# An attention and FP4 feed-forward block on one core: softmax row sums written to PSUM, the bias of q added in its copy, one copy moved from VectorE to ScalarE, and three PSUM banks in place of four

## What is computed

```python
mod = (silu(c) @ wmod).reshape(32, 6, 1, 128)            # sa, ca, ga, sb, cb, gb
h = layernorm(x) * (1 + ca) + sa
q, k, v = ((h @ W + b).reshape(b, 16, 8, 256) for each)
attn = softmax(einsum('bhdt,bhds->bhts', k, v) * temperature)
x = x + ga * einsum('bhdt,bhts->bhds', q, attn).reshape(b, 256, 128)
h = layernorm(x) * (1 + cb) + sb
# fp4_linear: both operands are rounded to FP4 in blocks of 16
hid = silu(fp4_linear(h, w_gate)) * fp4_linear(h, w_up)
x = x + gb * fp4_linear(hid, w_down)
```

## Time and profile before

| | |
|---|---|
| median of 3 runs | 613.16 us (612.82 to 613.65) |
| the profiled execution | 614.23 us |
| its span | 611.3 us, 15522 instructions |
| DVE busy | 568.7 us (93%) |
| PE busy | 558.3 us (91%) |
| ACT busy | 555.9 us (91%) |
| POOL busy | 507.3 us (83%) |
| one batch, from 118.03 to 547.63 us | 25 batches, 17.18 us each |

### The profile page before, as it was taken

One profiled execution on the slowest core, in us unless ns is written; L12 is line 12 of the kernel. 1 busy time (PEld: TensorE's weight loads), 2 busy tenths in 40 slices (PEclk: granted clock), 3 DMA queues, 4 the chain that ended last, 5 costly groups with the idle time before them and its releaser, 6 DMA issues.

```text
span 611.3 us, 15522 instructions
## 1 busy us (share of the span) xinstructions
PE 558.3 (91%) x4336; PEld 385.6 (63%) x4336; DVE 568.7 (93%) x1124; ACT 555.9 (91%) x2281; POOL 507.3 (83%) x710
## 2 busy tenths in 40 slices
PE   4588999999999999999999999999999999998874
PEld 2465556666666666666666666666666666666653
DVE  5568799999999999999999999999999999999986
ACT  2499899999999999999999999999999999999621
POOL 5544478999999999999999999999999999988741
PEclk9669899999999999999999999999999999999878
DMA  5655556546655556555655556655655556652000
GB/s 156 179 142 143 129 152 163 145 133 170 170 140 147 149 155 173 159 157 137 172 144 143 149 155 171 171 145 139 170 144 141 152 153 174 164 143 58 10 10 26
DMA packets 87888, 86.12 MB, mean 141 GB/s; under 512 B 8566, under 2 KB 83548, under 8 KB 87804
## 3 DMA queue, kind: packets, MB, share of 16 engines
q1 hardware_dynamic: 85372, 83.10, 50.4%
q10 hardware_dynamic: 2432, 2.03, 1.2%
HBM read 47.29 MB, written 37.81 MB: 139 GB/s over the span
## 4 chain that ended last, share of the span: by engine, by line
ACT 52%; PE 18%; issue 13%; DVE 12%; POOL 3%; ACTq 1%; DVEq 0%; POOLq 0%
ACT probs L825 47%; DVE neg_max L1005 6%; PE score_ps L1502 6%; PE bank L1581 5%; PE bank L1570 3%; ACT hT L835 2%; DVE silu_g L1123 2%; ACT hid_T L859 2%; PE bank L1548 2%; PE bank L1606 1%; ACT q_T L841 1%; DVE h_mag L975 1%; POOL hid_q L367 1%; PE bank L1520 1%; DVE h_mag L979 1%
## 5 line engine op out<-in xcount | busy, mean ns | idle before, releaser
L825 ACT ACTIVATE probs<-score_ps,neg_max 128x256 f32<-128x256 f32 x1024 | 483.5, 552 | 5.4 <-DVE neg_max L1005 4.3
L1005 DVE TENSOR_REDUCE neg_max<-score_ps 128x4 f32<-128x1024 f32 x256 | 312.1, 1219 | 19.5 <-PE score_ps L1502 16.8
L825 ACT ACTIVATION_READ_ACCUMULATOR probs<-score_ps,neg_max 128x1 f32 x1024 | 292.4, 286 | 0.0
L1502 PE MATMUL score_ps<-v_stack,k_stack 128*128 128x256 f32 x1024 | 234.9, 333 | 24.2 <-ACT probs L825 21.7
L1502 PEld LDWEIGHTS score_ps<-v_stack,k_stack 128*128 128x128 f32 x1024 | 156.0, 194 | 108.2 <-ACT probs L825 85.1
L1548 PE MATMUL bank<-probs,q_z 128*32 128x256 f32 x2048 | 132.6, 389 | 0.0
L1548 PEld LDWEIGHTS bank<-probs,q_z 128*32 128x32 f32 x2048 | 57.6, 111 | 42.4 <-issue 3.2
L1606 PEld LDWEIGHTS bank<-wd_T,hid_T 118*128 118x128 f32 x384 | 52.7, 201 | 7.6 <-ACT hid_T L859 1.3
L1606 PE MATMUL bank<-wd_T,hid_T 118*128 118x128 f32 x384 | 56.0, 286 | 0.5 <-ACT hid_T L859 0.5
L1570 PE MATMUL bank<-wgu_T,h_T 128*128 128x352 f32 x128 | 52.0, 488 | 1.7 <-ACT h_T L848 0.5
L367 POOL TENSOR_TENSOR hid_q<-hid_r,hid_sc 128x704 f32<-128x704 bf16 x31 | 43.0, 1387 | 7.6 <-DVE hid_r L362 7.5
(11 more groups left out here) (119 smaller groups left out, 880.9 us busy)
## 6 DMA issues: line engine op xcount, KB each, us to landing
split_dram<-kv_hi SPq DMA_DIRECT2D x124, 128.0 KB, 2.6
split_dram<-kv_lo SPq DMA_DIRECT2D x124, 128.0 KB, 2.6
k_stack<-split_dram SPq DMA_DIRECT2D x124, 128.0 KB, 4.5
...
x_in<-in_L_attn_x_dram SPq DMA_DIRECT2D x32, 128.0 KB, 3.1
out_dram<-out_t SPq DMA_DIRECT2D x32, 128.0 KB, 3.6
split_dram<-kv_hi ACTq DMA_DIRECT2D x4, 128.0 KB, 2.4
```

Of the source, the lines that this page charges most:

```text
L825: nc.scalar.activation(probs[p][:, h, a, :], score_ps[:, j % 4, a, :], ACT.Exp, bias=neg_max[:, p, n:n + 1], accum_out=row_sum[:, p, h, a: ...
L1005: nc.vector.tensor_reduce(neg_max[:, p, 4 * u:4 * u + 4], score_ps[:, lo:lo + 2, :, :].rearrange("p b a n -> p (b a) n"), AX.X, ALU.max, n ...
L1502: done = nc.tensor.matmul(score_ps[:, j % 4, a, :], k_stack[p][:, h, 128 * a:128 * a + 128], v_stack[p][:, h // R, :], start=True, stop=True)
```

## The change

Five things:

1. `bank_3` becomes ScalarE's own: the accumulated row sums go there (`row_ps`, 2 x 16 x 2 values). A new task on ACT, `row_sums_out`, copies the 32 columns of a batch to `row_sum` in SBUF, where `row_sums_inv` reads them as before. The last batch uses four quarter copies.
2. The bias of q is no longer a matmul: `q_out` becomes an Identity with a bias operand `b_q` of one value for each partition.
3. `v_hi` moves from DVE to ACT. `k_hi` on DVE then waits for it.
4. The rest shares three banks: bank_0 `x_transpose`, `q_proj`, `up_proj` 0, `mix`, `down_proj`; bank_1 `kv_proj`, `up_proj` 1, `hid_transpose` 1; bank_2 `h2_transpose`, `gate_proj` 0 and 1, `hid_transpose` 0. `gate_proj` 1 now waits for `silu` 0 of the same batch.
5. All five lists are in another order, the head and the `last` lists too.

```diff
-        b_raw = sb("b_raw", [64, 3 * D])
-        b_pad = sb("b_pad", [128, 3 * D], F32R)
-        ones_r = sb("ones_r", [128, T], F32R)
+        b_raw = sb("b_raw", [64, 2 * D])
+        b_q = sb("b_q", [128, 1])
+        b_pad = sb("b_pad", [128, 2 * D], F32R)
+        ones_r = sb("ones_r", [128, 128], F32R)
...
-        bank_xT, bank_kv, bank_q, bank_h2T, bank_mix, bank_down = bank_1, bank_1, bank_2, bank_0, bank_2, bank_3
-        bank_gate, bank_up, bank_hidT = (bank_2, bank_3), (bank_1, bank_0), (bank_2, bank_0)
-        bank_ffw = (bank_0, bank_3, bank_0)
+        bank_xT, bank_kv, bank_q, bank_h2T, bank_mix, bank_down = bank_0, bank_1, bank_0, bank_2, bank_0, bank_0
+        bank_gate, bank_up, bank_hidT = (bank_2, bank_2), (bank_0, bank_1), (bank_2, bank_1)
+        bank_ffw = (bank_1, bank_2, bank_2)
+
+        row_ps = bank_3[:, 0:2 * H * 2].rearrange("p (b h a) -> p b h a", b=2, a=2)
...
-                                         accum_out=row_sum[:, p, h, a:a + 1]).then_inc(exped, 1)
+                                         accum_out=row_ps[:, p, h, a:a + 1]).then_inc(exped, 1)
+
+            def row_sums_out(b, c):
+                if b == NB - 1:
+                    return
+                act.wait_ge(exped, 2 * H * (b + 1))
+                wait_batches(act, inv_made, b - 1)
+                nc.scalar.activation(row_sum[:, c % 2, :, :], row_ps[:, c % 2, :, :], ACT.Copy).then_inc(row_sums_made, 1)
...
+            def v_hi(b, c):
+                wait_batches(act, kv_ps_made, b + 1)
+                wait_dma(act, split_stored, b - 2, STORES * 16)
+                nc.scalar.activation(halves(kv_hi[c % 2][:, 1, :]), kv_rows(1), ACT.Copy).then_inc(v_hi_made, 1)
...
-                nc.scalar.activation(q_T[:, c, :, :], halves(bank_q[:, 0:T]), ACT.Copy).then_inc(qT_made, 1)
+                if b == 0:
+                    act.wait_ge(bq_in, 16)
+                nc.scalar.activation(q_T[:, c, :, :], halves(bank_q[:, 0:T]), ACT.Identity, bias=b_q[:, 0:1])\
+                    .then_inc(qT_made, 1)
...
             def k_hi(b, c):
-                wait_batches(dve, kv_ps_made, b + 1)
+
+                wait_batches(dve, v_hi_made, b + 1)
...
-            def v_hi(b, c):
-                wait_batches(dve, kv_ps_made, b + 1)
-                wait_dma(dve, split_stored, b - 2, STORES * 16)
-                nc.vector.tensor_copy(halves(kv_hi[c % 2][:, 1, :]), kv_rows(1)).then_inc(v_hi_made, 1)
...
             def row_sums_inv(b, c):
-                wait_batches(dve, exped, b + 1, 2 * H)
+                wait_batches(dve, row_sums_made, b + 1)
...
-                nc.tensor.matmul(bank_q[:, 0:T], w_q[:, :], hT[:, :], start=True, stop=False)
-                nc.tensor.matmul(bank_q[:, 0:T], b_pad[:, 0:D], ones_r[:, :], start=False, stop=True)\
-                    .then_inc(qT_ps_made, 1)
+                nc.tensor.matmul(bank_q[:, 0:T], w_q[:, :], hT[:, :], start=True, stop=True).then_inc(qT_ps_made, 1)
...
-                    wait_bank(b, [(ffn_g_made, b - 1)], (silu_made[1], b))
+                    wait_bank(b, [(silu_made[0], b + 1)], (h2T_made, b + 1), (hidT_made[0], b - 1), (silu_made[1], b))
```

More of the change, by code:

```diff
@@ new lines, in _ @@
+            last(hid_magic, 26)
+            last(v_lo, 31)
+            last(gate2, 25)
+            last(maxes, 29, 7)
+            last(k_hi, 31)
+            last(maxes, 30, 0)
+            last(h2_max, 28)
+            last(k_lo, 31)
+            last(silu, 27, 0)
+            last(row_sums_inv, 29)
+            last(maxes, 30, 1)
+            last(times_up, 27, 0)
+            last(h2_recip, 28)
+            last(silu, 27, 1)
+            last(maxes, 30, 2)
+            last(h2_exponent, 28)
@@ L1675, in _ @@
             last(scores, 31, 1)
+            last(gate_proj, 28, 0)
             last(up_proj, 28, 0)
[L1677 to L1678 removed]
             last(scores, 31, 2)
@@ L1687, in _ @@
             last(mix, 30, 3)
-            last(scores, 31, 6)
-            last(scores, 31, 7)
             last(mix, 30, 4)
```

648 lines of the change are left out of this document (372 added, 276 removed).

## The result

The changed kernel takes 630.19 us (median of 4 runs, 627.56 to 631.4), against 613.4 of the kernel before on the same chip (612.82 to 613.76): a ratio of 1.027, 95% interval 1.023 to 1.030. It is slower by 17 us, where the forecast was 10.6 us faster. The profiled execution took 631.4 us, with a span of 629.6.

The account below looks back on a forecast made before the run. ACT was taken to bound the kernel, DVE close behind; the change would make DVE bind. Batch 17.18 to 16.80 us saves 0.38, times 28 is 10.6: 613.16 to 602.5 us, own range 595.5 to 609, whole range 595 to 628.

Parts of the forecast that it names:

- ACT's side: On ACT, copies of v, q and row sums add 0.445 us a batch, paid for by 32 cheaper accumulator reads.
- s: Saving on each of ACT's 32 accumulator reads a batch when written to PSUM, taken as 0.03 to 0.05 us.
- the slope of the copies: ACT copies of 384 and 256 columns take 0.37 and 0.26 us; extrapolated to one column about 0.04, saving 0.05 a read.
- rival 1: On ACT, a read into PSUM costs what it costs now: batch 17.60 us, time 625 us; chance 0.22.
- three banks and new lists: Waits added by bank sharing and reordering leave DVE at most 0.25 us idle a batch: 16.60 to 16.85, taken as 16.80.
- 16.60: DVE's work a batch in us: 16.93 less 0.33 for the cast of v that goes to ACT.
- idle time past 0.25: On DVE, idle time growing past 0.25 us a batch was named as a sign that the forecast is wrong.
- Rival 2: Second gate projection waits for silu 0, stalling ACT up to 0.9 us a batch: 628 us, half stall 615; chance 0.11.
- Rival 3: Keys' way through DRAM, store to last landing, binds: 0.3 us longer makes batch 17.1, 611 us (608 to 616); chance 0.12.
- The head and the end: First and last batches: mended POOL wait against earlier memsets and a maximum, summed as 0 with 2 us either way.
- PE's matmul: On PE, one matmul of 0.496 us a batch goes; costed at nothing since PE waits 2.2 us for exponentials.

Follow-up runs that it names:

- 3: The changed kernel with the row sums accumulated into an SBUF tile instead of bank_3; 641.87 us, ratio 1.049 to the kernel before.
- 1: The changed kernel with hid_magic moved behind variance1 on VectorE and residual2 behind h2_sub on GpSimd; 614.23 us, ratio 1.004 to the kernel before.
- the first kernel of 6: On top of 1, on VectorE: variance1 between stats2_rows and variance2, k_hi between hid_exponent and hid_magic; 613.2 us, ratio 1.001 to the kernel before.
- 5: On top of 1: variance1 and silu 1 moved on VectorE, 619.31 us; kv_proj ahead of down_proj 0 on TensorE, 623.07; both plus k_hi moved, 622.63.

## Why the prediction was wrong

*ACT's side was right.* The read costs 0.04 less; the copies of v, of q and of the sums take 0.28, 0.40 and 0.07 us where 0.26, 0.36 and 0.09 were taken. That s lies in the middle of its range is in part luck: the slope of the copies, which led to it, says nothing of the destination, and 3 shows that the destination makes it. With s = 0.04 its sum was 17.15 + 0.445 - 32 x 0.04 = 16.3 us; from the distances in 1, 32 x 0.41, two `tanh` at 0.39, two `hidT_out` at 0.39, and 0.45, 0.40, 0.32, 0.28 and 0.07 for the rest, it is 16.2. It stopped being the bound, and rival 1 fell. (Its busy share in 1, 98.7%, says otherwise: the 0.51 us of an exponential run on under its read and its successor, so an ACT that pauses by 0.1 between pairs still counts as busy.)

*The step that failed* is the one on "three banks and new lists": "in the forecast I let them keep DVE as idle as it is now, at most: 0.25 us". With 16.60 for DVE's list this gave 16.80. In after DVE is busy 17.22 us a batch and idle 0.43, which is the 17.65; the prediction had named idle time past 0.25 as a sign of being wrong. It had two faults. The 16.60 took every DVE duration from the trace of before, as if a duration belonged to the instruction; but two 16-bit instructions of 0.28 and 0.33 us took 0.44 and 0.59 on average, because the new lists start them while a POOL instruction runs. And the idle time grew to 0.43, with ACT waiting for maxima and POOL for a store. Both follow from where two lines stand in two lists. Moving them back (1) took 0.61 us off the batch.

*Even then the batch was 17.05, not 16.80.* In 1 DVE has hardly a wait left (those over 0.15 us sum to 0.6 in 420; its other 5.2 us of idle time are shorter gaps between neighbours), so I take its list as what binds, and the list itself is longer than 16.60. By the distance from start to start, before and in 1: `stats2_rows` 0.29 and 0.45, `hid_magic` 0.25 and 0.39, `h2_exponent` 0.21 and 0.31, `gate2` 0.30 and 0.37, `k_lo` 0.50 and 0.56; `times_up` gives back 2 x 0.03. That is 0.47 more, and 16.6 + 0.47 is the batch. The first and the third are a neighbour that reads what the instruction writes: in the list of before something stood between. The second is what is left of the collision, now with `normalise2`; without it (the first kernel of 6) the distance is 0.25. Where neighbours were parted, DVE's list got shorter only in the first of 6, to 16.8 us, and `k_hi`'s wait for ACT took the place: 17.06. In 5 the batch rose to 17.3 and 17.4. What order of the lists would give 16.8 is open.

*Rival 2, both gates in one bank*, did not hold: after's waits show no stall of the second `tanh` for `gate_proj` in each batch, and 1 is even with that bank still shared. *Rival 3*, the way through DRAM, did not bind in any steady batch. Neither named what happened. The 628 us at the upper edge of the range stood for most of rival 1 and for the full stall of rival 2; that the real time lies within 3 us of it owes nothing to either.

*The head and the end* together were put at 0 with 2 us either way; they lost 3.2 and 3.4. The mended wait of the earlier trace rows did not help, since memsets and a maximum ahead of the first norm delayed the first `hT` from 7.21 to 10.20 us. Of the end 2.5 us are still lost in 1, from `gate1` of batch 29 on (63.6 us against 61.2), and no run says to what.

*PE's matmul* was put at nothing. No run puts it back, so that is not tested; PE is busy 16.6 us a batch in both kernels.
